# A kernel of a Mamba tower: the first chunk's rows normalised in pairs, the bulk loads put behind the second chunk's rows, and 88 unread products on TensorE before the first projections

## What is computed

```python
x = emb[input_ids]
for i in range(N_LAYER):
    x = x + _mamba_block(_rmsnorm(x, norm_w[i]), in_proj_w[i], ...)
def _rmsnorm(x, w):
    return x * jax.lax.rsqrt(jnp.mean(x * x, axis=-1, keepdims=True) + EPS) * w
def _mamba_block(...):
    xz = x @ in_proj_w
    xr, res = jnp.split(xz, 2, axis=-1)
    xc = conv_general_dilated(xr, conv_w, ...)      # 4 taps, each channel by itself
    xr = jax.nn.silu(xc + conv_b)
    ...
```

## Time and profile before

| what | us |
|---|---|
| median of 3 timed runs | 372.81 |
| lowest and highest | 370.98 to 373.37 |
| the profiled execution, own time | 370.15 |
| its span, first to last instruction | 368.3 |
| PE, DVE, ACT, POOL busy | 298.6, 301.1, 286.5, 201.6 |

### The profile page before, as it was taken

The page is one execution under the profiler, slowest core; times in us unless marked ns, Lnnn a source line. Parts: engine busy times, 40 slices in busy tenths (PEclk is TensorE's granted clock), DMA queues, the critical chain, the costliest instruction groups (busy, mean ns, idle before and its releaser), DMA issues.

```text
span 368.3 us, 6291 instructions
## 1 busy us (share of the span) xinstructions
PE 298.6 (81%) x1714; PEld 167.9 (46%) x1714; DVE 301.1 (82%) x772; ACT 286.5 (78%) x596; POOL 201.6 (55%) x190
## 2 busy tenths in 40 slices
PE   0099966995688897886879689899999999998784
PEld 0144422323246362325553337574856774666443
DVE  3037899979979999999899997973557598899997
ACT  2349999867799889899995989865657996897663
POOL 6753035983586955747978739546103334247460
PEclk9999995799999999998999999999999999999869
DMA  6993000000000000000000000000000000000012
GB/s 156 112 285 86 1 2 0 0 3 0 0 2 1 1 2 0 2 0 2 1 0 4 0 0 4 3 0 2 1 3 2 2 1 2 13 13 21 12 36 84
DMA packets 7135, 7.88 MB, mean 21 GB/s; under 512 B 1643, under 2 KB 6138, under 8 KB 7098
## 3 DMA queue, kind: packets, MB, share of 16 engines
q1 hardware_dynamic: 5464, 5.71, 5.2%
q0 software_dynamic: 768, 1.57, 3.3%
q10 hardware_dynamic: 866, 0.17, 0.2%
HBM read 5.87 MB, written 1.57 MB: 20 GB/s over the span
## 4 chain that ended last, share of the span: by engine, by line
PE 33%; DVE 20%; issue 17%; POOL 15%; ACT 13%; DMA 1%; DVEq 0%; ACTq 0%; POOLq 0%
PE bank L1014 5%; POOL du L1871 4%; POOL pair L1877 3%; DVE arena L2210 3%; PE bank L1146 3%; PE bank L1115 3%; PE bank L1195 3%; PE bank L1159 3%; POOL arena L1865 3%; PE bank L1020 2%; PE bank L1181 2%; POOL arena L1883 2%; DVE arena L2223 2%; PE bank L1118 2%; DVE pair L2180 2%
## 5 line engine op out<-in xcount | busy, mean ns | idle before, releaser
L1014 PE MATMUL bank<-ring,win 128*128 128x512 f32 x96 | 51.9, 676 | 17.4 <-ACT ring L384 5.6
L2180 DVE SCALAR_TENSOR_TENSOR pair<-bank,cw,pair 128x504 f32<-128x504 f32 (+2 forms) x72 | 51.1, 737 | 9.5 <-ACT pair L337 7.2
L1883 POOL TENSOR_TENSOR arena<-arena 128x512 f32<-128x512 f32 x24 | 37.0, 1546 | 31.7 <-DVE arena L2223 19.2
L1865 POOL TENSOR_TENSOR arena<-arena,dl 128x512 f32<-128x512 f32 x24 | 32.6, 1364 | 36.1 <-DVE dl L2172 34.3
L1096 PE MATMUL bank<-wout,pair 128*128 128x192 f32 x192 | 37.7, 353 | 7.5 <-DVE arena L2204 2.6
L1096 PEld LDWEIGHTS bank<-wout,pair 128*128 128x128 f32 x192 | 34.0, 205 | 13.2 <-issue 4.7
L1014 PEld LDWEIGHTS bank<-ring,win 128*128 128x128 f32 x96 | 18.5, 211 | 43.6 <-issue 20.0
L1871 POOL TENSOR_TENSOR du<-dl,pair 128x512 f32<-128x512 f32 x24 | 32.1, 1349 | 2.7 <-DVE dmin L2189 2.7
L2210 DVE TENSOR_TENSOR_SCAN arena<-arena 128x512 f32<-128x512 f32 x24 | 31.2, 1309 | 0.0
L1877 POOL TENSOR_TENSOR pair<-pair,arena 128x512 f32<-128x512 f32 x24 | 30.2, 1276 | 0.0
L1902 POOL TENSOR_TENSOR pair<-pair,gout 128x512 f32<-128x512 f32 x16 | 20.8, 1300 | 11.4 <-DVE pair L2390 5.8
(11 more groups left out here) (175 smaller groups left out, 832.4 us busy)
## 6 DMA issues: line engine op xcount, KB each, us to landing
out<-h SPq DMA_DIRECT2D x16, 96.0 KB, 1.6
win<-in_w SPq DMA_DIRECT2D x2, 384.0 KB, 3.8
arena<-ffn_in_t SPq DMA_DIRECT2D x1, 768.0 KB, 8.1
wout<-out_w SPq DMA_DIRECT2D x2, 288.0 KB, 3.5
win_rest<-in_w SPq DMA_DIRECT2D x2, 192.0 KB, 3.5
arena<-ffn_out_t SPq DMA_DIRECT2D x1, 384.0 KB, 9.1
wa<-w_qkv SPq DMA_DIRECT2D x1, 384.0 KB
h<-emb,idx POOLq DMA_INDIRECT x16, 5.6
```

The costliest lines, as they stand in the source:

```text
L1014: nc.tensor.matmul(bank[:, IN_BANKS[j][m], :], win[:, j // NG, m * P:(m + 1) * P], xtr[:, j % 2, i, :], start=True, stop=False)
L1865: nc.gpsimd.tensor_tensor(relu_s[:, c, :], relu_s[:, c, :], dl[:, j % NG, c, :], ALU.subtract).then_inc(rest_done, 1)
L1883: nc.gpsimd.tensor_tensor(yv[:, c, :], yv[:, c, :], bx[:, c, :], ALU.add).then_inc(yv_done, 1)
L2180: nc.vector.scalar_tensor_tensor(acc, seqs(bank[:, IN_BANKS[j][c], :])[:, :, 0:LEN - tap], cw[:, j // NG, c, TAPS - 1 - tap:TAPS - tap], a ...
```

## The change

- Chunk 0's rows are squared, raised, rooted and scaled in two pairs (`square_first`, `raise_first`, `root_inverse_first`, `scale_first`), with a semaphore of its own for the first two rows, and transposed in pairs (`turn_first`).
- POOL issues two rows of chunk 1 ahead of pair 0's root, one between the two roots and one after them.
- SP's bulk loads wait for all of chunk 0's and chunk 1's rows.
- DVE's `weight_magnitudes` moves from ahead of the first convolution to behind the fourth.
- PE issues 88 products of `ident` with `ones`, 128 columns each, in float32, into a bank that nobody reads before it is overwritten: 68 ahead of pair 0's transposes, 12 between the pairs, 8 between the last transposes and the wait for the evictions. The first 68 wait for nothing but the constants and `prep`.
- Counts of later waits move by one because chunk 0 now counts twice.

```diff
--- before.py
+++ after.py
@@ -203,6 +203,7 @@
         ld_ids, ld_rate, ld_in, ld_xp, ld_out, ld_late = (
             sem(n) for n in ("ld_ids", "ld_rate", "ld_in", "ld_xp", "ld_out", "ld_late"))
         wx_ready = sem("wx_ready")
+        first_rows = sem("first_rows")
         gathered = [sem(f"gathered{g}") for g in range(NG)]
         const_ready, ident_zero, pad_ready, steps_clear, one_rows_ready, prep, rate_step = (
             sem(n) for n in ("const_ready", "ident_zero", "pad_ready", "steps_clear", "one_rows_ready", "prep", "rate_step"))
@@ -273,7 +274,9 @@
                 sp.dma_start(wdt[at + DT_IN + R:at + STEP_ROWS, :, cols], dt_b.rearrange("(a l) n -> a l n", a=1)[:, :, cols])\
                     .then_inc(ld_xp, 16)
             sp.dma_start(wout[:, 0, :, :], out_w[0].rearrange("(c p) n -> p c n", p=P)).then_inc(ld_out, 16)
-            sp.wait_ge(gathered[0], 16 * SG)
+            sp.wait_ge(first_rows, 32)
+            sp.wait_ge(gathered[0], 32)
+            sp.wait_ge(gathered[1], 16 * SG)
             sp.dma_start(win_f.rearrange("p (k n) -> p k n", k=KH), ffn_in_t.rearrange("(k p) n -> p k n", p=KP))\
                 .then_inc(ld_f, 16)
             sp.dma_start(wout_f.rearrange("p (c n) -> p c n", c=FC), ffn_out_t.rearrange("(c p) n -> p c n", p=P))\
@@ -394,7 +397,7 @@
 
             def square_sums(j):
                 g = j % NG
-                act.wait_ge(gathered[g], 16 * SG)
+                act.wait_ge(gathered[g], 16 * SG if g else 32)
                 if j >= NG:
                     act.wait_ge(h_added, 2 * (j - NG) + 2)
                 if j >= 2:
@@ -404,8 +407,20 @@
                     nc.scalar.activation(xsr[:, j % 2, i, :], h[:, t, :], ACT.Square,
                                          scale=D ** -0.5, accum_out=ms[:, t:t + 1]).then_inc(ms_ready, 1)
 
+            def square_first(half):
+                act.wait_ge(gathered[0] if half else first_rows, 32)
+                for i in (2 * half, 2 * half + 1):
+                    nc.scalar.activation(xsr[:, 0, i, :], h[:, i, :], ACT.Square,
+                                         scale=D ** -0.5, accum_out=ms[:, i:i + 1]).then_inc(ms_ready, 1)
+
+            def scale_first(half):
+                act.wait_ge(rstd_ready, half + 1)
+                for i in (2 * half, 2 * half + 1):
+                    last = nc.scalar.activation(xsr[:, 0, i, :], h[:, i, :], ACT.Identity, scale=rstd[:, i:i + 1])
+                last.then_inc(xs_ready, 1)
+
             def scale(j):
-                act.wait_ge(rstd_ready, j + 1)
+                act.wait_ge(rstd_ready, j + 2)
                 for i in range(SG):
                     t = j % NG * SG + i
                     last = nc.scalar.activation(xsr[:, j % 2, i, :], h[:, t, :], ACT.Identity, scale=rstd[:, t:t + 1])
@@ -553,8 +568,10 @@
                 nc.scalar.activation(yt[:, s % 2, :, :], bank[:, TH_BANKS[s], :].rearrange("p (c n) -> p c n", c=FC),
                                      ACT.Identity, bias=neg_rne[:, :]).then_inc(yt_ready, 1)
 
-            square_sums(0)
-            scale(0)
+            square_first(0)
+            square_first(1)
+            scale_first(0)
+            scale_first(1)
             take_xt(0, 0)
             take_xt(0, 1)
             square_sums(1)
@@ -993,12 +1010,20 @@
                 nc.tensor.matmul(bank[:, WSUM_BANK, 0:2], ones[:, :], wsum[:, :], start=True, stop=True)\
                     .then_inc(wtot_ready, 1)
 
-            def keep_clock(n, b):
+            def raise_clock(n):
                 for _ in range(n):
-                    nc.tensor.matmul(bank[:, b, 0:P], ident[:, :], ident[:, :], start=True, stop=True)
+                    nc.tensor.matmul(bank[:, IN_BANKS[0][5], 0:P], ident[:, :], ones[:, :], start=True, stop=True)
+
+            def turn_first(half, k):
+                pe.wait_ge(xs_ready, half + 1)
+                for i in (2 * half, 2 * half + 1):
+                    last = nc.tensor.transpose(bank[:, T_BANKS[0][k], i * LEN:(i + 1) * LEN],
+                                               xsr[:, 0, i, k * (D - P):k * (D - P) + P], ident[:, :])
+                if half:
+                    last.then_inc(tr_ready, 1)
 
             def turn_in(j, k):
-                pe.wait_ge(xs_ready, j + 1)
+                pe.wait_ge(xs_ready, j + 2)
                 for i in range(SG):
                     last = nc.tensor.transpose(bank[:, T_BANKS[j][k], i * LEN:(i + 1) * LEN],
                                                xsr[:, j % 2, i, k * (D - P):k * (D - P) + P], ident[:, :])
@@ -1210,8 +1235,13 @@
                                             start=(c == 0), stop=(c == FC - 1))
                 last.then_inc(dn_ready, 1)
 
-            turn_in(0, 0)
-            turn_in(0, 1)
+            raise_clock(68)
+            turn_first(0, 0)
+            turn_first(0, 1)
+            raise_clock(12)
+            turn_first(1, 0)
+            turn_first(1, 1)
+            raise_clock(8)
             pe.wait_ge(xt_ready, 2)
             project_in(0, 0)
             project_in(0, 1)
@@ -1849,13 +1879,18 @@
 
             pool.wait_ge(idx_ready, 1)
 
-            def gather(g):
-                for s in range(g * SG, (g + 1) * SG):
+            def gather(g, rows=range(SG)):
+                for s in (g * SG + i for i in rows):
                     nc.gpsimd.indirect_dma_start(
                         out=h[:, s, :], out_offset=None, in_=emb,
-                        in_offset=bass.IndirectOffsetOnAxis(ap=idx[:, s:s + 1], axis=0)).then_inc(gathered[g], 16)
+                        in_offset=bass.IndirectOffsetOnAxis(ap=idx[:, s:s + 1], axis=0)).then_inc(gathered[g] if s >= 2 else first_rows, 16)
+            def root_inverse_first(half):
+                pool.wait_ge(ms_raised, half + 1)
+                t = slice(2 * half, 2 * half + 2)
+                nc.gpsimd.tensor_tensor(rstd[:, t], ms[:, t], neg_half[:, t], ALU.pow).then_inc(rstd_ready, 1)
+
             def root_inverse_in(j):
-                pool.wait_ge(ms_raised, j + 1)
+                pool.wait_ge(ms_raised, j + 2)
                 t = slice(j % NG * SG, (j % NG + 1) * SG)
                 nc.gpsimd.tensor_tensor(rstd[:, t], ms[:, t], neg_half[:, t], ALU.pow).then_inc(rstd_ready, 1)
 
@@ -1927,8 +1962,11 @@
                 nc.gpsimd.memset(va[b][:, :, :, HD:HD + 1], 1.0).then_inc(ones_col, 1)
 
             gather(0)
-            gather(1)
-            root_inverse_in(0)
+            gather(1, (0, 1))
+            root_inverse_first(0)
+            gather(1, (2,))
+            root_inverse_first(1)
+            gather(1, (3,))
             gather(2)
             root_inverse_in(1)
             gather(3)
@@ -2154,6 +2192,11 @@
                 dve.wait_ge(wstep, 11)
 
 
+            def raise_first(half):
+                dve.wait_ge(ms_ready, 2 * half + 2)
+                t = slice(2 * half, 2 * half + 2)
+                nc.vector.tensor_scalar(ms[:, t], ms[:, t], EPS_RMS, None, ALU.add).then_inc(ms_raised, 1)
+
             def raise_squares(j):
                 dve.wait_ge(ms_ready, 4 * j + 4)
                 t = slice(j % NG * SG, (j % NG + 1) * SG)
@@ -2428,13 +2471,14 @@
                                                ALU.mult, ALU.add).then_inc(h_out, 1)
 
             dve.wait_ge(prep, PREP)
-            raise_squares(0)
+            raise_first(0)
+            raise_first(1)
             raise_squares(1)
-            weight_magnitudes()
             convolve(0, 0, 1)
             convolve(0, 1, 1)
             convolve(0, 0, 2)
             convolve(0, 0, 3)
+            weight_magnitudes()
             raise_squares(2)
             convolve(0, 1, 2)
             convolve(0, 1, 3)
```

## The result

The changed kernel takes 383.85 us (median of 4 executions, 380.49 to 387.78), the kernel before 371.89 in the runs beside them: a ratio of 1.031, 95% interval 1.025 to 1.037, so 11.7 us slower. The profiled execution is the fastest of the four (380.49 against 370.15 before, +10.3). Some executions of a kernel are slow ones, with a lower granted clock; no ratio here counts them, and where the only profile of a kernel is of one ("sums back in their gap", "pairs alone"), its head alone is used.

A forecast was written before the change was run, and what follows sets the result against it. No engine was taken to bound the whole span, with TensorE, then ScalarE and VectorE, full after 27 us. Profiled 370.15 + 6.3 (products) + 1.5 (weight sums) = 378.0, or 379.6 us from the mean of executions; range 374.5 to 385.5.

The forecast's parts named there:

- The price of a product: TensorE at the head: a float32 product is two records, 0.213 us each at the low clock, 0.107 at the upper.
- The low level: TensorE's first products run at the lower clock for 5.1 us, 24 records; ends none to 7.9 us.
- First transposes at 24.1, projections at 29.3, the line behind at 32.75: TensorE at the head: 68 products delay the transposes; L1020 comes 6.3 us late, ends 3.7 to 7.7.
- The pairs are worth nothing: Chunk 0's rows are scaled at 16.2, 1.2 us earlier, but TensorE is busy with its 68 products until 24.1.
- Loads, gathers, chunk 1 at zero: Bulk loads from 21, last gathers at 32 to 37 and chunk 1's later rows all land in time, costing zero.
- Sums, 1.5 us: Weight sums behind four convolutions stall TensorE about 1.6 us before project_in(1, 1); cost 1.5 us, ends 0 and 3.2.
- The delay is kept to the end: Work late before 27 us meets no slack until long after; matmuls stay in order, so 6.3 us stands in full.
- Sum: Whole kernel: 6.3 plus 1.5 us gives 378.0 profiled, 379.6 from the mean of executions; ends 375.5 to 382.7.
- the 3 us allowed for the clock falling once more: Upper margin of the 374.5 to 385.5 range: 3 us for the clock falling once more than before.
- Rival 1: The low-clock stretch beginning at 56 us doesn't come back: 2.8 us less, 376.8 us; chance 0.20.
- Rival 2: Head products cost one record each: L1020 2.45 us early, 1.0 us faster in all, 370.8 us; chance 0.08.
- rival 3: Unread products don't raise the clock: all 176 records take 0.213 us, 26 us late, 397 us; chance 0.05.

The follow-up runs named there:

- sums back in their gap: Changed kernel with the weight sums back ahead of VectorE's first convolution, all 88 products kept: ratio 1.034 (1.024 to 1.044) to the kernel before.
- pairs alone: Kernel before with only the pairs and their order of gathers; no products, bulk loads and weight sums where they were: ratio 1.004 (0.999 to 1.008).
- 28 products again: Second profile of the changed kernel with 19, 3 and 6 float32 products in place of 68, 12 and 8: one execution, no ratio, span 373.4 us.
- 7 wide ones: Changed kernel with 5, 1 and 1 products of 512 columns in place of 68, 12 and 8 of 128: ratio 0.997 (0.993 to 1.000).
- 28 short: Changed kernel with 19, 3 and 6 float32 products in place of 68, 12 and 8: ratio 1.012 (1.006 to 1.018).
- The two kernels with 7 wide products: Changed kernel with 5, 1 and 1 products of 512 columns, ratio 0.997; the same with weight sums two convolutions later, ratio 0.998.
- the one with 12: Changed kernel with 8, 1 and 3 products of 512 columns in place of 68, 12 and 8 of 128: ratio 1.000 (0.995 to 1.005).
- the three profiles that choke: Changed kernel with sums back in their gap (1.034), with the 88 products in bfloat16 (1.012), and 28 short (1.012).
- the repeat: The changed kernel run again unaltered, also called the second profile: ratio 1.022 (1.012 to 1.033), 379.84 to 385.84 us.
- Products alone: Kernel before with only the products, 68 ahead of turn_in(0, 0) and 20 behind turn_in(0, 1): ratio 1.022 (1.011 to 1.033).

## Why the prediction was right, and where it was short

- **The price of a product** (0.21 us at the upper level): right. 24 records take 2.84 us with a last one of 0.275, so (2.84 - 0.275)/23 = 0.1115 a record, 0.22 a product. My 0.107 was 4% low, which over some 110 records is 0.5 us.
- **The low level** (5.1 us taken, 0 to 7.9 allowed): 5.9 in one profile, about 3 in the other. That the two lie on either side of 5.1 is luck: 5.1 was taken from one profile.
- **First transposes at 24.1, projections at 29.3, the line behind at 32.75** (6.3 late): measured 25.2, 30.54, 34.07 (7.6 late), and 32.68 (6.2) in the second profile.
- **The pairs are worth nothing**: right, pair 1 was scaled 10 us before even the first transposes (25.20). It was there earlier than I worked out (15.3, not 16.2).
- **Loads, gathers, chunk 1 at zero**: right in this kernel; the loads started at 18.4, not 21. The cover is thin, as the quicker kernels show: 28 products again found VectorE waiting 1.26 us for the weights, and 7 wide ones ScalarE waiting 2.04 us for chunk 2's rows.
- **Sums, 1.5 us**: 1.2 to 1.3, by the mechanism given (a stall ahead of project_in(1, 1) of 1.6 forecast, 1.23 measured).
- **The delay is kept to the end**: right, 8.9 at 46 us and 8.5 at 355 us.
- **Sum**: 7.8 us forecast; 8.9 and 7.5 as shift in the two profiles. The measured ratios are 11.7 us (9.4 to 13.9) and 8.2 us (4.3 to 12.2). What the sum lacked is the column "rest", +1.5 and +2.9 in those two. I had taken it as zero, with a rival that made it negative. The median of 383.85 lies above 382.7, the sum of all upper ends; it falls in the range of 374.5 to 385.5 through the 3 us allowed for the clock falling once more, for which no row stood.
- **Rival 1** (the low clock from 56 us doesn't come back) fell: in every profile a stretch of 13.7 us at the lower clock begins between 51 and 69 us. Before and in the changed kernel, the clock (third number from the right) is the same over 18 us laid round it:

```profile
52.00:70.00 18.00, 12.38 (x27) 4.10 (x28) 17.25 (x33) 16.85 (x34) 13.17 (x11) 0.62 0.00 1
```

```profile
60.00:78.00 18.00, 11.90 (x25) 3.73 (x24) 17.31 (x33) 17.40 (x35) 13.04 (x10) 0.62 0.00 0
```

- **Rival 2** (one record a product) and **rival 3** (the clock never rises) fell by the records themselves. One figure of rival 2 was a slip: its own sum goes from 1.0 us faster at 0.107 us a product to 7.8 slower at 0.214, and so changes sign at about 0.12, not 0.15.

## What to carry to other kernels

Unread products on an in-order engine are real work: they must end when the data arrive, so count records of 128 columns (a float32 product is two) times 0.11 or 0.21 us, by the clock level, against the length of the gap, here 7 us, into which 15 to 29 us of them were put. All that warming could ever give was 3.6 us. The best placed version was 2.5 us early at 46 us, where the kernel without any products was already 1.1 early, and the timed runs resolve neither. A delay ahead of a stretch in which every engine is full is paid in full at the end, and a piece of work taken out of a gap can cost in the full stretch: 3.2 us of sums cost 1.3 us there.

## What the runs showed that I had not expected

**Short records can choke.** With 56 to 176 records of 128 columns ahead of the projections, some executions have gaps of 0.3 to 1.1 us between records with no wait in the program, or a semaphore that arrives 6 us late, between 12 and 22 us, while GpSimd issues gathers. The same kernel (28 short) had it in one profile and not in the next; 88 float32 products had it in one of four (sums back). The two kernels with 7 wide products (14 records) and the one with 12 (24 records) had none. Gathers and loads alone don't make it: in the changed kernel the gathers run to 20.7 and the loads start at 18.4, as in the three profiles that choke, and no record is late. Instruction fetches in flight don't either: in those three no packet of an instruction queue moves between 12 and 22 us, and in the changed kernel one does, at 19.5. All three are free again between 22.1 and 22.3 us. What stands behind it is open.

**Where the clock falls later moves the time by some us.** The two profiles of the changed kernel, the same program in the same stretch, the first run ahead of the repeat:

```profile
158.00:215.00 57.00, 46.24 (x163) 25.39 (x163) 54.01 (x100) 49.04 (x86) 43.93 (x33) 0.94 0.00 1
```

```profile
158.00:215.00 57.00, 45.84 (x155) 23.57 (x155) 51.87 (x94) 46.78 (x82) 41.83 (x32) 0.89 0.00 1
```

With a mean clock of 0.89 against 0.94 the repeat gets fewer records done. Against the kernel before, the table load that stands there at 125.60 is 8.8 us late in the first run and 7.1 in the repeat; the one at 236.93 is 8.5 and 10.1 late. At the end it is the first run that loses 1.9 us and the repeat 0.3. That both have a span of 378.7 is chance. Products alone lose in both places, 2.6 us and then 1.9, which is their rest of +4.6. The single execution of 28 short, again, has a clock of 0.76 from 150 to 215 us, where the kernel before has 0.95; its table loads are 1.1 us early at 153 us and 5.0 late at 242. Clock and loss go together in all of these; why the clock falls in one execution and not in the next isn't shown. A difference of 1% between two versions of this kernel is therefore read from a fixed event early in the list, and from many executions, rather than from one span.
